# Last layer of a 2-layer model: the shared expert's products move behind the experts' blocks, its additions go in tile by tile

## The reference

```
scores = sigmoid(x @ w_router); 4 of 8 groups are kept, then 8 of 64 experts
topk_w = 2.5 * scores[topk] / sum(scores[topk])
x_sorted = x_flat[sort by expert]
o = ragged_dot(silu(ragged_dot(x_sorted, we_gate)) * ragged_dot(x_sorted, we_up), we_down)
y = zeros.at[token].add(o * topk_w)                    # 8 rows for each token
shared = (silu(x @ ws_gate) * (x @ ws_up)) @ ws_down   # every token, F = 128
x = x + y + shared
```

## Time and profile before

| what | us |
|---|---|
| median of 3 runs | 2411.56 (2410.48 to 2414.87) |
| profiled execution, its own time | 2412.86 |
| its span in the trace | 2411.2 |
| router of layer 1, first DVE step to last | 1700.8 to 1843.1 |
| blocks, first gather to last DVE copy | 1844.4 to 2224.4 |
| ending, to the last DVE step | 2224.4 to 2408.0 |

### The profile page before, as it was taken

The page is one execution under the profiler, slowest core; times in us unless marked ns, Lnnn a source line. Parts: engine busy times, 40 slices in busy tenths (PEclk is TensorE's granted clock), DMA queues, the critical chain, the costliest instruction groups (busy, mean ns, idle before and its releaser), DMA issues. The chain is left out here.

```text
span 2411.2 us, 38801 instructions
## 1 busy us (share of the span) xinstructions
PE 1873.5 (78%) x11288; PEld 1301.1 (54%) x11289; DVE 1563.1 (65%) x3375; ACT 1024.7 (42%) x2930; POOL 1241.5 (51%) x1000
## 2 busy tenths in 40 slices
PE   5699978888888668999579999699548999988000
PEld 5378843343433243677437878588414888876000
DVE  5599928999999968333537777477686333333633
ACT  1467637666656323333037777343215333332000
POOL 1488616766666610788305555366002554543775
PEclk9799988999999977999879999899665999999555
DMA  7311013212111052998511110100503999998332
GB/s 211 96 73 73 8 44 130 102 40 93 48 72 69 0 166 60 230 294 199 141 34 32 32 37 24 29 1 2 188 0 98 286 282 281 275 252 202 110 116 84
DMA packets 163804, 272.04 MB, mean 113 GB/s; under 512 B 28722, under 2 KB 97300, under 8 KB 162708
## 3 DMA queue, kind: packets, MB, share of 16 engines
q1 hardware_dynamic: 130708, 199.72, 25.4%
q0 software_dynamic: 30464, 68.19, 12.4%
q10 hardware_dynamic: 2496, 2.44, 0.4%
HBM read 218.74 MB, written 51.53 MB: 112 GB/s over the span
## 5 line engine op out<-in xcount | busy, mean ns | idle before, releaser
L1017 POOL TENSOR_TENSOR b_h<-b_h,b_bcb 128x1024 f32<-128x1024 f32 x128 | 301.9, 2358 | 151.4 <-DVE b_h L1074 150.8
L1573 POOL DMA_INDIRECT m1x_xb<-scratch_xn,m_tok x192 | 183.0, 953 | 330.9 <-DVE m1x_yb L1702 173.7
L842 PE MATMUL b_psy<-b_h,ident 128*128 128x512 f32 x512 | 252.8, 621 | 69.5 <-POOL b_h L1017 69.2
L1074 DVE TENSOR_TENSOR_SCAN b_h<-b_dA,b_pbx 128x1024 f32<-128x1024 f32 x128 | 292.6, 2286 | 4.4
L1620 PE MATMUL m1x_psh<-m1x_xe,m1x_w 128*128 128x128 f32 x1536 | 211.8, 282 | 23.8 <-DMA m1x_w<-in_m_w 20.9
L1689 DVE TENSOR_TENSOR m1x_hT<-m1x_sg,m1x_psh 128x128 f32<-128x128 f32 x192 | 55.2, 287 | 240.3 <-ACT m1x_sg L1672 143.9
L1620 PEld LDWEIGHTS m1x_psh<-m1x_xe,m1x_w 128*128 128x128 f32 x1536 | 190.7, 195 | 34.5 <-issue 22.2
L842 PEld LDWEIGHTS b_psy<-b_h,ident 128*128 128x128 f32 x512 | 93.6, 194 | 210.3 <-POOL b_h L1017 123.3
L973 ACT ACTIVATE b_dA<-b_delta,b_A 128x504 f32<-128x504 f32 x256 | 166.8, 706 | 93.3 <-DVE b_h L1074 87.8
L1883 POOL TENSOR_TENSOR x_s<-x_s,x_rs 128x1024 f32<-128x1024 f32 x64 | 121.1, 1893 | 127.5 <-DVE x_rs L2049 127.4
L1068 DVE TENSOR_TENSOR b_pbx<-b_pdx,b_bcb 128x1024 f32<-128x1024 f32 x128 | 157.6, 1231 | 20.9 <-ACT b_pdx L956 14.8
(11 more groups left out here) (449 smaller groups left out, 4401.6 us busy)
## 6 DMA issues: line engine op xcount, KB each, us to landing
m1x_w<-in_m_w SPq DMA_DIRECT2D x192, 256.0 KB
b_bcb<-scratch_bc_rows SPq DMA_DIRECT2D x64, 512.0 KB, 4.8
scratch_y<-m1x_yb SPq DMA_DIRECT2D x192, 128.0 KB
m_w<-in_m_w SPq DMA_DIRECT2D x64, 368.0 KB
a_c<-in_ctxT SPq DMA_DIRECT2D x16, 512.0 KB, 3.6
m_w<-in_m_w SPq DMA_DIRECT2D x64, 128.0 KB
x_c<-in_ctxT SPq DMA_DIRECT2D x32, 256.0 KB
m_w2all<-in_m_w SPq DMA_DIRECT2D x1, 8192.0 KB
```

The source lines that it names most:

```text
L842: mm = pe.matmul(psy[:, k % 2, :], ident[:, :], h[:, u % HB, j, :], start=False, stop=(nq == NQ - 1 and j == CQ - 1))
L1017: q.tensor_tensor(hs, hs, bcb[:, 1, CQ * nq:CQ * nq + CQ], ALU.mult).then_inc(sem("hc"), 1)
L1074: v.tensor_tensor_scan(h[:, u % HB].rearrange("p j n -> p (j n)"), dA[:, u % DB].rearrange("p j n -> p (j n)"), pbx[:, :, :].rearrange("p ...
L1573: g.indirect_dma_start(out=xb[:, j, :], out_offset=None, in_=xn, in_offset=bass.IndirectOffsetOnAxis(ap=tok[:, b:b + 1], axis=0)).then_inc ...
```

## The change

In layer 1 no unit of the shared expert is made in the router any more. Its four units are made behind the last block: PE issues unit g ahead of `shared_output` of tile 4g, ACT has the four `shared_silu` behind the blocks, and DVE gates unit g just ahead of the addition of tile 4g. DVE now makes the weights first, and the 16 additions (L1718 before) no longer come ahead of them in one run: each is done just ahead of the eight weighted rows of its own tile. A wait on `x_added` is put between the addition and the weighted rows of each tile. Layer 0's program stays as it is.

```diff
-    FIRST, SECOND = (2, 7) if capped else (2, 4)
+    FIRST, SECOND = (2, 7) if capped else (0, 0)
...
-                    pe.wait_ge(rs("hs"), FIRST)
+                    if FIRST:
+                        pe.wait_ge(rs("hs"), FIRST)
...
                     if not capped:
                         pe.wait_ge(rs("ebc"), 1)
-                        pe.wait_ge(rs("hs"), SECOND)
...
-                    shared_gated(v, FIRST, gate_up(FIRST)[1])
+                    if FIRST < SECOND:
+                        shared_gated(v, FIRST, gate_up(FIRST)[1])
...
-            EARLY, LATE = (range(SECOND, SECOND + 3), range(SECOND + 3, UNITS)) if capped else ((), ())
+            EARLY = range(SECOND, SECOND + 3) if capped else ()
+            LATE = {2 * n: SECOND + 3 + n for n in range(2)} if capped else {4 * g: g for g in range(NG)}
...
                     for t in range(NT):
-                        if t % 2 == 0 and t // 2 < len(LATE):
-                            units(LATE[t // 2])
+                        if t in LATE:
+                            units(LATE[t])
                         shared_output(t)
...
-                    for m in LATE:
+                    for m in LATE.values():
                         shared_silu(a, m, pgu[0])
...
-                    for t in range(NT):
-                        if t % 2 == 0 and t // 2 < len(LATE):
-                            shared_gated(v, LATE[t // 2], pgu[1])
+
+                    def shared_added(t):
+                        if t in LATE:
+                            shared_gated(v, LATE[t], pgu[1])
                         v.wait_ge(xs("out"), t + 1)
                         v.tensor_tensor(X[:, t, :], X[:, t, :], pso[t % 4][:, 0:D], ALU.add).then_inc(xs("x_added"), 1)
-                    v.wait_ge(xs("x_added"), NT)
+
+                    if capped:
+                        for t in range(NT):
+                            shared_added(t)
+                        v.wait_ge(xs("x_added"), NT)
...
                     for t in () if capped else range(NT):
                         u, n = t % RB, t // RB
+                        shared_added(t)
+                        v.wait_ge(xs("x_added"), t + 1)
                         v.wait_ge(xs("yg", u), 16 * K * (n + 1))
```

## The result

The changed kernel took 2423.81 us (median of 6 runs, 2421.72 to 2426.34), the kernel before 2413.22 (6 runs beside them, 2409.73 to 2418.82). The ratio is 1.0044, interval 1.0031 to 1.0058: slower by 10.6 us (7.5 to 14). Forecast were 2430 us and, at a chance of 0.54, a slower kernel. The total is near; what it is made of is not, as the profile shows first. For one of its terms, the blocks, the experiments then show the cause.

A forecast was written before the change was run, and what follows sets the result against it. The prediction took transfers to bound the blocks and DVE's slow pace, not POOL, to set the end. Router -6.5 and ending +24.8 summed to +18.3 us, giving 2430 us on the median, range 2389 to 2442.

The forecast's parts named there:

- The router: Ahead of the blocks: without the units' gatings on DVE, it gets 6.5 us shorter, between 4 and 7.
- The part for L1442: In the router: DVE's L1442 starts 5.3 us earlier because PE's rank matmuls no longer wait for the gating.
- The blocks start as much earlier and, bound by transfers, end as much earlier: In the block loop: it only moves earlier by the router's 6.5 us, its length unchanged.
- The sum: Over the whole kernel: router -6.5 and ending +24.8 make +18.3 us, giving 2430 us.
- The ending: Behind the blocks, from tile 3 on: 163 us in place of 138.4, +24.8, as DVE runs more instructions.
- PE's output waits: In the ending: behind each of three gatings DVE waits about 2 us for PE's output, 6 together.
- slow pace: DVE's weighted rows in the ending, unexplained: 1.38 us a step for 103 steps, assumed to hold for 103 again.
- The slow pace is gone: Rival, in the ending: without the pace POOL's gathers set the end at 10.1 us a tile; about 2393 us, chance 0.38.
- PE's output is the new wait: Rival, in the ending: additions wait for `shared_output`; at 5 us each, 9 us more; cannot decide alone, no chance given.

The follow-up runs named there:

- first comparison: The changed kernel against the kernel before, six timed runs each and one profile of each, chip not recorded: 2423.81 against 2413.22 us, ratio 1.0044.
- before_exp: The kernel before with a one-column Exp on ACT ahead of the block loop, against the kernel before on chip 12: 1.0034, +8.1 us.
- after_silu: The changed kernel with a one-column Silu on ACT ahead of the block loop, against the kernel before on chip 12: 0.9968, -7.7 us.
- pad32: The kernel before with 32 one-column memsets on DVE ahead of its block loop, against the kernel before on chip 7: 1.0007.
- pad96: The kernel before with 96 one-column memsets on DVE ahead of its block loop, against the kernel before on chip 13: 0.9997, -0.7 us.
- before_again: The kernel before, unchanged, run once more on chip 12 for its profile: one run, 2401.81 us.
- early_gating: The changed kernel with all four units multiplied and gated while DVE makes the weights, against the kernel before on chip 7: 1.0017, +4.1 us.
- after_again: The changed kernel, unchanged, run once more against the kernel before on chip 12: 1.0017, +4.1 us.

## Why the prediction was right or wrong

**The router: right.** Forecast 6.5 us, bounds 4 to 7; 7.1 in the first comparison, 6.7 on chip 12. The part for L1442 was forecast at 5.3 and came to 1.20 + 10.27 - 5.92 = 5.55 us: the two gatings are gone, and the wait for ranks fell from 5.29 to 0.94 us.

**"The blocks start as much earlier and, bound by transfers, end as much earlier": wrong, and this is the step that failed.** I costed the four Silu as free to move ("ACT's four Silu likewise"), looking at their durations and not at what they leave behind. The last of them left Silu's table loaded when ACT entered the block loop. With it gone, the last load ahead of the blocks is that of the router's Exp, and the loop has a load ahead of its first Copy and one ahead of its first Silu in each of 23 rounds, as before_exp has behind its one-column Exp. The blocks are longer by 6.9 us in the first comparison, by 10.9 on chip 12 and by 6.2 in before_exp's profile; its timed runs are longer by 8.1. The sum had 0 for it and said "I see nothing for it". The load at L1168 was in the trace of before, ahead of a moved instruction, and would have been the thing to ask about. The prediction also said that a longer block loop would upset everything. It did: the blocks took back what the router gave.

The Trainium skill has two places on this. "ScalarE: Activation LUTs", section "What ACT_TABLE_LOAD costs", gives about 1283 ns for a load, and the trace agrees with 1283. The page adds about 1380 ns of drain for every switch, 2.66 us in all, by which 46 loads would keep ACT for an estimated 122 us. The trace doesn't show the drain: the next activation starts 1.30 us behind the load's start (1866.31, 1867.61), which makes 60 us. "ScalarE activation tables: per-element evaluation and per-set limits", section "Table sets in the compiler and the runtime", says that the back end places loads per block of the program. That both loads stand in the loop's body, once in every round, fits that; that one activation ahead of the loop brings them in or takes them out is what before_exp and after_silu show.

**The ending: the direction right, the size wrong.** Forecast +24.8 us from tile 3 on, 163 in place of 138.4; measured 2417.33 + 4.13 - 2278.09 = 143.4, or +5.0. The pace did hold for about as many instructions again: from 2290.96 to 2414.92 DVE has 81 weighted rows, 10 additions with 10 waits on `x_added`, and 2 gatings, 103 in all. What was mis-sized is, first, where it begins: I let it begin with tile 3, and it began 12.9 us behind that, in tile 4, so the instructions ahead of it were hidden by POOL's gathers. Second, its pace: 123.96/103 = 1.20 us and not 1.38, since an addition and the wait behind it, which I counted as two, cost about one step together. Tiles 5 to 7 start their rows at 2298.66, 2311.26 and 2323.86, 12.6 us apart, where 11.2 was the pace before; that a tile would take 12 to 14 us in the slow stretch was forecast and came out. PE's output waits were forecast at 2 us and show 3.00, 3.69 and 2.98; the one of tile 4 was covered by the gathers. All this is in one profile of each kernel, and no experiment met the slow pace again.

**What the slow pace is: open.** It was in both profiles of the first comparison and in none of the twelve of the experiments, on three chips, two of them of the kernel before and one of the changed kernel. It is therefore not a property of either program alone, as the sum had treated it. Whether it is a property of a chip or of a time, and whether it sits at a place in DVE's program, pad32 and pad96 could not tell. One rival was not tested: the fetching of instructions. In both slow profiles the core's instruction queue moves an 8 KB packet less than 2 us ahead of the first slow step (between 2260 and 2261 in the kernel before, between 2289 and 2290 in the kernel after). But before_again has such a packet between 2260 and 2261 too, and no slow pace behind it. The kernel before took 2413 us beside it and 2396 to 2400 on the others: 14 to 18 us; between its first profile and before_again's the endings (183.5 and 172.1) account for 11.4 and the blocks (367.6 and 361.7) for 5.9, while before_again came to the router 8.3 us later.

**The rivals.** "The slow pace is gone" came about on three chips, with POOL at 10.2 us a tile as that rival said, but it was absent from the kernel before as well, so the change won nothing by it: 1.0017 and not the 0.992 of that rival's 2393 us. "PE's output is the new wait" is real in the first comparison (the three waits above) and hidden where there is no slow pace: early_gating takes those waits out and has 1.0017 on chip 7, as the changed kernel itself has on chip 12. That the forecast of 2430 came near 2423.8 is thus luck in good part: one term was 20 us too large and one of 7 us was missing. With the measured terms (-7.1, +6.9, +5.2) the same sum gives 2411.6 + 5.0 = 2416.6, and the 7 us up to 2423.8 are in none of its terms.

## What to carry to other kernels

When an activation is moved out of a stretch, ask which table it left loaded for what follows, above all for a loop: a load that moves into a loop is paid in every round. Look for ACT_TABLE_LOAD in the trace of before beside each activation that moves. One activation of one column, put into ACT's idle time ahead of the loop, turned a change of +4 us into one of -5 to -8 on two chips.

A stage that is "bound by transfers" has only some margin for its engines, and it can be read: here eight blocks took mostly 13.5 to 15.5 us without loads and 15 or more with two loads in them, so the margin was used up. And a slowdown that no wait explains should be looked for in a second execution before it is put into a sum.

## What the runs showed of the hardware

- A pace of DVE at which steps of 0.48 us start 0.7, 1.4 or 2.1 us apart was there in both profiles of one comparison and absent from twelve profiles on three chips, with the same rows at 0.52 us apart.
- Two table loads of 1.283 us in eight blocks delay the next `yb` copy by 1.75 us (3.37 in place of 1.62), and not by 2.57: in the same timeline of after_again ACT waits 0.4 to 0.6 us for PE ahead of most Copies and 0.51 us ahead of each Silu without a load, and the loads take up that time.
- In pad32 and pad96 the router took 139.8 and 139.5 us in place of 141.1 to 141.5, though its own instructions were the same; no run here says why.
